# An attention and expert layer on one core: a third PSUM bank for scores, side work moved between the couples of a unit

## What is computed

```python
xn = layernorm(x)
q, k, v = xn @ Wq.T, xn @ Wk.T, xn @ Wv.T      # 16 heads of 8
q, k = rope(q), rope(k)
att = softmax(q k.T / sqrt(8)) v               # per batch and head, 512 x 512
# router, 32 experts in 8 groups of 4
scores = sigmoid(xn @ gate_w.T); sc = scores + e_bias
# keep the 4 groups with the largest sum of their top 2, then the top 6 experts
w = 2.5 * scores[top6] / (sum(scores[top6]) + 1e-20)
moe = sum_e w_e * (relu(xn @ up_e.T)**2 @ down_e.T)      # 64 wide each
shared = relu(xn @ shared_up.T)**2 @ shared_down.T       # 256 wide
out = x + att + moe + shared
```

## Time and profile before

| | |
|---|---|
| median of 3 runs | 724.7 us (721.32 to 726.27) |
| profiled execution | 720.83 us, of which the span is 719.0 |
| PE busy | 692.2 us, 96% of the span |
| DVE busy | 489.1 us, 68%; row maxima 330.9 in 512 |
| ACT busy | 407.4 us, 57%; exponents 278.0 in 512 |
| POOL busy | 397.8 us, 55% |
| mean granted clock of TensorE | 0.958 |

### The profile page before, as it was taken

The page is one execution under the profiler, slowest core; times in us unless marked ns, Lnnn a source line. Parts: engine busy times, 40 slices in busy tenths (PEclk is TensorE's granted clock), DMA queues, the critical chain, the costliest instruction groups (busy, mean ns, idle before and its releaser), DMA issues. The chain is left out here.

```text
span 719.0 us, 12483 instructions
## 1 busy us (share of the span) xinstructions
PE 692.2 (96%) x4450; PEld 326.5 (45%) x4450; DVE 489.1 (68%) x1179; ACT 407.4 (57%) x771; POOL 397.8 (55%) x337
## 2 busy tenths in 40 slices
PE   7979899999999999999999999999999999999996
PEld 7523344444544454444544454445444453445443
DVE  5872467858786788668765788668786878565400
ACT  2522445566656655566646656566656656665663
POOL 1660135665575656565654657565665555566554
PEclk9985589999999999999979999999999999999999
DMA  7816033353236334643424334643435423332320
GB/s 192 261 61 179 3 88 90 106 163 91 73 80 206 90 89 118 206 94 89 114 59 156 90 89 119 205 94 89 118 85 177 97 55 95 93 89 60 89 60 15
DMA packets 52973, 77.78 MB, mean 108 GB/s; under 512 B 6064, under 2 KB 19248, under 8 KB 52784
## 3 DMA queue, kind: packets, MB, share of 16 engines
q1 hardware_dynamic: 52336, 75.95, 40.3%
q10 hardware_dynamic: 576, 1.05, 0.4%
HBM read 57.19 MB, written 19.40 MB: 107 GB/s over the span
## 5 line engine op out<-in xcount | busy, mean ns | idle before, releaser
L629 DVE TENSOR_REDUCE nmax<-sc 128x1 f32<-128x512 f32 x512 | 330.9, 686 | 173.2 <-PE sc L799 170.5
L455 ACT ACTIVATE probs<-st 128x512 f32<-128x512 f32 x512 | 278.0, 595 | 161.3 <-PE st L815 161.2
L349 POOL TENSOR_TENSOR gated<-gate_at,relu 128x512 f32<-128x512 f32 x128 | 163.6, 1278 | 272.4 <-ACT relu L460 272.4
L832 PEld LDWEIGHTS acc<-dn,g 128*128 128x128 f32 x1024 | 136.3, 192 | 128.0 <-issue 124.9
L832 PE MATMUL acc<-dn,g 128*128 128x128 f32 x1024 | 175.8, 295 | 1.4 <-POOL g L353 1.4
L353 POOL TENSOR_TENSOR g<-gated,relu 128x512 f32<-128x512 f32 x128 | 163.0, 1273 | 18.5 <-POOL gated L349 0.4
L799 PE MATMUL sc<-stacks 32*128 32x512 f32 x512 | 154.6, 509 | 14.1 <-DVE nmax L629 12.4
L815 PE MATMUL st<-stacks 32*128 32x512 f32 x512 | 151.4, 586 | 0.0
L826 PE MATMUL pv<-probs,v_aug 128*32 128x512 f32 x1024 | 139.0, 615 | 0.0
L854 PE MATMUL upb<-xnT,up 128*128 128x512 f32 x256 | 134.0, 606 | 0.0
L460 ACT ACTIVATE relu<-upb 128x512 f32<-128x512 f32 x128 | 76.3, 596 | 83.8 <-PE upb L854 83.8
(11 more groups left out here) (107 smaller groups left out, 445.8 us busy)
## 6 DMA issues: line engine op xcount, KB each, us to landing
gate_at<-gate_rows SPq DMA_DIRECT2D x64, 512.0 KB, 6.7
q_stack<-qk_parts SPq DMA_DIRECT2D x32, 256.0 KB, 6.6
stacks<-q_stack SPq DMA_DIRECT2D x32, 256.0 KB, 3.0
stacks<-k_stack SPq DMA_DIRECT2D x32, 256.0 KB, 3.5
k_stack<-qk_parts SPq DMA_DIRECT2D x28, 256.0 KB, 5.6
gate_at<-in_x SPq DMA_DIRECT2D x8, 256.0 KB, 5.1
x_res<-in_x SPq DMA_DIRECT2D x8, 256.0 KB, 7.2
out<-y SPq DMA_DIRECT2D x8, 256.0 KB, 7.1
```

Source lines behind the costliest of these rows:

```text
L349: nc.gpsimd.tensor_tensor(gated[:, u % 2, :], gate_at[:, group % RING, u % GATES, :], relu[:, u % RELUS, :], ALU.mult).then_inc(gated_read ...
L455: nc.scalar.activation(probs[:, u % 2, h, :], st_b[h % 2][:], ACT.Exp).then_inc(probs_ready, 1)
L629: nc.vector.tensor_reduce(out=nmax[:, s % 2, at:at + 1], in_=sc_b[i % 2][:], op=ALU.max, axis=AXX, negate=True).then_inc(s_read, 1)
L832: m = nc.tensor.matmul(acc_b[:, t * P:(t + 1) * P], src[:, t * P:(t + 1) * P], weights, start=first and t == 0, stop=end, skip_group_check ...
```

## The change

- `tr` becomes a third bank for scores, `sc2`. Tile t uses bank t % 3 and waits for row maximum t-3.
- All that was written to `tr` is written to `upb`. It stands between pv and the second couple. TensorE waits before it for relu of u-1 and before up for its evacuation. ACT evacuates it between exponents 1 and 2, as it does the attention's `pv` bank.
- The attention transpose moves from kt = 2 to kt = 1, the max transpose from kt = 1 to kt = 2, shared ups to units 3 and 7, the gate transpose to 11, v to 15, the shared downs to 2 and 3. POOL's finish of a batch moves from unit 4 to 3.
- down is issued whole, behind the second couple.
- DVE: the cut stands behind the row maxima of the units with kt = 1; the attention part in the middle of them. Router pieces: 2, 3, 5 and 6 (max8 and match_replace) stand in the middle of units 3, 4, 6 and 7; 0, 1, 4, 7 and 8 at the end of units 0, 2, 4, 7 and 8. Two tensor_scalar operations move from pieces 3 and 6 to pieces 4 and 7.
- The prelude writes all transposes of x to `upb`, so that x 3 waits for the evacuation of x 2, and x 5 for that of v.

```diff
@@ banks and units
-                for n in ("sc0", "sc1", "st0", "st1", "pv", "upb", "tr", "acc")]
+                for n in ("sc0", "sc1", "sc2", "st0", "st1", "pv", "upb", "acc")]
-        V_UNIT, SH_UNIT, GATE_UNIT = 3, (7, 11), 12
-        MAX_KT, ATT_KT = 1, 2
-        SHDOWN_UNIT = (4, 5)
+        SH_UNIT, GATE_UNIT, V_UNIT = (3, 7), 11, 15
+        ATT_KT, MAX_KT = 1, 2
+        CUT_KT = 1
+        SHDOWN_UNIT = (2, 3)
-        SUM_UNIT, Y_UNIT = 2, 4
+        SUM_UNIT, Y_UNIT = 2, 3
+        ROUTE_MID, ROUTE_END = {3: 2, 4: 3, 6: 5, 7: 6}, {0: 0, 2: 1, 4: 4, 7: 7, 8: 8}
@@ ACT, a unit
-                for h in range(QUAD):
-                    exponent(u, h)
+                exponent(u, 0)
+                exponent(u, 1)
                 if kt == 0 and q:
                     att_evac(q - 1)
                 if kt == MAX_KT and q + 1 < STEPS:
                     max_rows(q + 1)
...
+                exponent(u, 2)
+                exponent(u, 3)
@@ DVE, a unit
-                for h in range(QUAD):
...
+                if n == SUM_UNIT and b:
+                    add_residual(b - 1)
+                for tile in SC_AT[u, 0] + SC_AT[u, 1]:
+                    row_max(tile)
+                if kt == ATT_KT and q:
+                    att_out(q - 1)
+                if n in ROUTE_MID and b + 1 < B:
+                    route(b + 1, ROUTE_MID[n])
+                for tile in SC_AT[u, 2] + SC_AT[u, 3]:
+                    row_max(tile)
+                if kt == CUT_KT and q + 1 < STEPS:
+                    cut_max(q + 1)
+                if n in ROUTE_END and b + 1 < B:
+                    route(b + 1, ROUTE_END[n])
@@ TensorE
-                wait(pe, s_read, tile - 1)
-                nc.tensor.matmul(sc_b[i % 2][:], stacks[rows_of(h), s % NQ, 0, qt * P:(qt + 1) * P],
+                wait(pe, s_read, tile - SC_BANKS + 1)
+                nc.tensor.matmul(sc_b[tile % SC_BANKS][:], stacks[rows_of(h), s % NQ, 0, qt * P:(qt + 1) * P],
...
             def expert_up(u):
+                b, n, kt, q = u // SLICES, u % SLICES, u % TT, u // TT
                 wait(pe, relu_ready, u)
+                if kt == ATT_KT and q:
+                    pe.wait_ge(atty_ready, q)
+                if kt == MAX_KT and q + 1 < STEPS:
+                    pe.wait_ge(m_ready, q + 2)
+                if b + 1 < B:
+                    if n in SH_UNIT:
+                        pe.wait_ge(sh_relu, (b + 1) * NSH + SH_UNIT.index(n) + 1)
+                    if n == GATE_UNIT:
+                        pe.wait_ge(gT_ready, b + 2)
+                    if n == V_UNIT:
+                        pe.wait_ge(v_ready, b + 2)
...
             for u in range(UNITS):
                 b, n, kt, q = u // SLICES, u % SLICES, u % TT, u // TT
...
+                couple(u, 0)
+                if u:
+                    pv(u - 1)
+                wait(pe, relu_ready, u)
+                if kt == ATT_KT and q:
+                    att_transpose(q - 1)
                 if kt == MAX_KT and q + 1 < STEPS:
...
                     max_transpose(q + 1)
...
                     if n in SH_UNIT:
                         shared_up(b + 1, SH_UNIT.index(n))
                     if n == GATE_UNIT:
                         gate_transpose(b + 1)
+                    if n == V_UNIT:
+                        make_v(b + 1)
+                couple(u, 2)
+                if u >= LAG:
+                    expert_down(u - LAG)
                 if n in SHDOWN_UNIT:
                     shared_down(b, SHDOWN_UNIT.index(n))
-                if u >= LAG:
-                    expert_down(u - LAG, 1)
                 expert_up(u)
```

More of the change, by code:

```diff
@@ L47 @@
 LAG = 2
+SC_BANKS = 3
 AHEAD = 12
@@ L448, in gate_out @@
                 wait(act, gate_stored, b * 16)
-                nc.scalar.activation(gT[:, :], tr_b[0:NE, :], ACT.Copy).then_inc(gT_ready, 1)
+                nc.scalar.activation(gT[:, :], up_b[0:NE, :], ACT.Copy).then_inc(gT_ready, 1)
             def exponent(u, h):
@@ L471, in _ @@
                     act.wait_ge(xnT_psum, i + 1)
-                    nc.scalar.activation(xnT[:, i * T:(i + 1) * T], turn_b(i)[:], ACT.Copy
+                    nc.scalar.activation(xnT[:, i * T:(i + 1) * T], up_b[:], ACT.Copy
                                          ).then_inc(xnT_ready, 1)
@@ L715, in transpose_x @@
                     pe.wait_ge(xn_pool, POOL_LN.index(i) + 1)
-                if i >= 2:
-                    pe.wait_ge(xnT_ready, i - 1 if i < 4 else i)
+                wait(pe, xnT_ready, i)
+                if i == 5:
+                    pe.wait_ge(v_ready, 1)
                 if i == 6:
@@ L720, in transpose_x @@
                 for t in range(TT):
-                    last = nc.tensor.transpose(turn_b(i)[:, t * P:(t + 1) * P], xn[:, i * TT + t, :], ident[:])
+                    last = nc.tensor.transpose(up_b[:, t * P:(t + 1) * P], xn[:, i * TT + t, :], ident[:])
                 last.then_inc(xnT_psum, 1)
@@ L776, in gate_transpose @@
                 for t in range(TT):
-                    m = nc.tensor.transpose(tr_b[0:NE, t * P:(t + 1) * P], gates[:, t, :], ident[:])
+                    m = nc.tensor.transpose(up_b[0:NE, t * P:(t + 1) * P], gates[:, t, :], ident[:])
                 m.then_inc(gate_turned, 1)
@@ L816, in weights_product, with couple @@
                                  stacks[rows_of(h), j, 0, :], start=False, stop=True).then_inc(t_done, 1)
+            def couple(u, h):
+                for k in (h, h + 1):
+                    weights_max(u, k)
+                for k in (h, h + 1):
+                    weights_product(u, k)
+                for tile in SC_AT[u, h] + SC_AT[u, h + 1]:
+                    score(tile)
             def pv(u):
@@ L828, in pv, with down_slice @@
                 m.then_inc(pv_done, 1)
-            def down_slice(src, weights, first, end, tiles=range(TT)):
-                for t in tiles:
+            def down_slice(src, weights, first, end):
+                for t in range(TT):
                     m = nc.tensor.matmul(acc_b[:, t * P:(t + 1) * P], src[:, t * P:(t + 1) * P], weights,
@@ L834, in down_slice, with expert_down @@
                 return m
-            def expert_down(u, half):
+            def expert_down(u):
                 b, n = u // SLICES, u % SLICES
-                if half == 0:
-                    pe.wait_ge(g_ready, u + 1)
-                    if n == 0:
-                        wait(pe, sum_ready, b)
-                last = down_slice(g[:, u % 2, :], dn[:, n, :], n == 0, n == SLICES - 1,
-                                  range(half * TT // 2, (half + 1) * TT // 2))
-                if half:
-                    last.then_inc(down_done, 1)
+                pe.wait_ge(g_ready, u + 1)
+                if n == 0:
+                    wait(pe, sum_ready, b)
+                down_slice(g[:, u % 2, :], dn[:, n, :], n == 0, n == SLICES - 1).then_inc(down_done, 1)
             def shared_down(b, i):
@@ L876, in prelude @@
                     if i == 0:
[L877 removed]
+                        pe.wait_ge(xnT_ready, 6)
                     else:
@@ L904, in _ @@
                 b, n, kt, q = u // SLICES, u % SLICES, u % TT, u // TT
-                for h in range(0, QUAD, 2):
-                    weights_max(u, h)
-                    weights_max(u, h + 1)
-                    weights_product(u, h)
-                    weights_product(u, h + 1)
-                    for tile in SC_AT[u, h] + SC_AT[u, h + 1]:
-                        score(tile)
-                    if h == 0:
-                        if u:
-                            pv(u - 1)
-                        if u >= LAG:
-                            expert_down(u - LAG, 0)
```

78 lines of the change are left out of this document (19 added, 59 removed).

## The result

The changed kernel takes 694.3 us, the median of four runs (688.47 to 699.01). The kernel before took 723.0 on the same chip (718.48 to 726.27). The ratio is 0.958, with a 95% interval of 0.949 to 0.967; it is that of the fast runs, which leaves out the run of 699.01. The prediction was 692, with a range of 668 to 712.

What follows compares the result with a forecast made beforehand. TensorE's own work was taken to bound the kernel, with score waits for DVE and clock falls on top. 719.0 - 25.7 + 2.0 - 1.7 + 0.5 - 4.5 = 689.6; 691.4 with 1.8 around, plus 1: 692, range 668 to 712.

Steps and rivals of the forecast that it cites:

- What bounds it: Whole kernel: TensorE's own work bounds it, with only scores waiting for DVE and TensorE's lower clock on top.
- The stalls removed: Third bank and moved DVE pieces remove score waits: unit 9 17.0, unit 2 4.7, rest 1.5, units 0 to 3 2.5; 25.7 us.
- DVE's residue: Unit 9's cut still ends late beside POOL, so unit 10's second couple waits: 2.0 us taken, bounds 1.2 to 8.
- list of queues: Moved DMAs, gate stores and POOL's earlier finish of a batch were claimed to delay nothing: 0.
- (D): Rival: DVE's waits only move, router pieces at five unit ends meeting POOL; 14 us lost, 705 us, chance 0.13.
- The order: TensorE's units with down whole, couple after pv and the exponents' wait: plain +0.04, max -0.1 each; net -1.7 us.
- The new wait: Second couple's maxima wait for the first couple's exponents, behind ACT's relu; its second member starts at 1.79: 0.24 us.
- Units 0 to 3 and the prelude: Score waits at half clock in units 0 to 3 go, -2.5 us; prelude transposes wait for evacuations, +0.5.
- (B): Rival: the clock also stays up through the prelude, worth 20 us: 672 us, chance 0.17.
- The clock in the steady part: The clock's fall at 368 us goes, as no array stands behind the cut: -4.5 us.
- (C): Rival: the second couple's wait costs 0.24 plus 0.55 in 67 units: 726 us, 731 with a clock fall; chance 0.10.
- (E): Rival: the change does nothing, as bank waits were hidden anyway: 719 to 725 us, chance 0.05.

Runs made afterwards that it cites:

- The best kernel: Changed kernel with POOL's splits, squares and final sum moved, v's second-buffer fills early, identity transposes of 12, 10, 12 and 8 in TensorE's stands: 668.32 us, ratio 0.9285.

## Why the prediction was right, and which of its terms were not

The span was to come out at 689.6 and came out at 692.7. That it came so close is partly luck: one term was 9.5 too small, and others were off the other way. Step by step:

- **What bounds it.** Right. The plain unit of after is TensorE's own work end to end, and with POOL moved, with no wait for DVE left, a batch is 74.55, against 74.86 for before's batch with its three stalls taken off (78.40 - 2.43 - 0.78 - 0.33).
- **The stalls removed, 25.7.** Unit 9 went from 6.85 to 4.65 and unit 2 from 5.42 to 5.18, though it now has a shared down (0.89) and a max transpose in place of the attention's: both stalls gone whole. How it came about was seen less well. The forecast books it under the third bank, and the moved pieces with it, without dividing. Two banks with the new DVE order cost 1.1 a batch at the higher clock, three banks with the old one 1.9, both together 3.4; the larger part is DVE's order.
- **DVE's residue, 2.0.** This is the term that was wrong: 11.5. Two parts. *Unit 10*: the value taken was 0.2 in six batches, the measured one 1.27, 7.6 in all, at the upper bound of 8. The step took the cut's end to be 1.2 us into unit 10, since both slow operations of the earlier trace rows got in at the first gap, each once. In the run three operations waited one after the other, each for one of three POOL operations that follow each other without a gap. The sentence "misses the gap and waits for the next one" had the right price, 1.3, and was set aside; its way there was another, one operation that waits twice. It named the wrong victim too: the max transpose waits for the cut first, at its place between the couples, not the second couple's score. *Unit 5*: 0.65 in six batches, 3.9, not in the sum at all. The change moves POOL's final sum to where piece 4 runs, and the forecast gave that move 0 in its list of queues: it asked whether the sum's inputs were there, not what it would run beside. Rival (D) had this mechanism, with "POOL is free from 3.5 to 5.0 in the new unit" against it. It is not free there in unit 4 (the final sum, 3.4 to 4.7), nor in units 6 to 9 (the splits) and 14 (a square), though only units 4 and 9 made the next one late.
- **The order, -1.7.** Right, with its working. Down whole 0.99 (1.0 forecast), pv into a couple 0.99 (no more than into a down), plain unit 4.28 (4.28), max unit 4.29 (4.32). The stall-free batch fell by 0.31, 2.4 in 7.7 batches. The bound of a whole further couple did not come: the couple takes 0.55 and the lateness, as the earlier trace rows said.
- **The new wait, 0.24.** Its size is right and its cause half so. The forecast lets ACT's relu go first; with relu behind, the exponents still end at 1.74, as they wait for the products.
- **Units 0 to 3 and the prelude.** -2.5 + 0.5 = -2.0 forecast, -6.1 measured, all of it before up of unit 0. The fall near 47 came as in the forecast, but from 63.7 to 70.5 us the clock was back. From the score at 61.24 to up of unit 0 the same work takes 10.84 us where it took 14.79 (from the score at 63.38), so the clock's return is worth 3.95 of the 6.1. Why it came back is open: before had the array shown busy in all of 60 to 70 us, and stayed at 0.50. The other 2.1 were there earlier: the score that starts at 61.24 is that much ahead of before's. With the third bank TensorE does the second shared up at 43.38, ahead of the stand and at the higher level. Before it came at 46.95, behind the stand, and took 2.04 at the lower level. The forecast saw this move, but only in (B), and gave it no price; its 2.5 were for waits in units 0 to 3. Those went too, by about the right size: units 1 to 3 take as long as before with 1.6 us more of work in them (at the higher level; more at the lower). So the 4.1 that the sum lacks are gains ahead of unit 0 that it did not price.
- **The clock in the steady part, -4.5.** Measured 4.3, in batch 3. That the fall goes with the stand was argued from one case. The experiments bear it out: all eleven falls between up 3 and up 127, in the twelve traces of this case, come at most 1.9 us after the end of a stand of 0.84 to 1.54 us, and the kernels without such a stand there have none. With the stalls gone and the stands of the start filled, the clock stays up everywhere.
- **The rivals.** (B) did not happen. TensorE did go on to the second shared up, as it says (43.38), but the score behind it came at 46.80 and had stood 2.29, not 1.7, and the clock fell. The 20 that it gave for a prelude at the higher level, on top of the forecast's 2.0, was a little high: with the stands filled, up of unit 3 comes 13.3 us sooner than in after, and 19.4 sooner than before. The best kernel's span is 14.1 below that of the kernel with POOL alone moved (681.0 to 666.9, the memset's move in it). (C) did not happen: the couple costs 0.55 and the lateness, 0.79, and a batch without stalls is shorter than before's. Its sum was also off a little: 67 x 0.55 less 1.7 is 35, not 33. The mark that the prediction set for (C), a second couple that takes longer than 0.6, was badly put, for its own forecast makes it 0.55 + 0.24 when counted from the first member (1.54) and 0.55 only from the second (1.78). (E) fell with the waits. (D) holds 11.5 of the 14 that it was priced at, though in two units instead of five, and its mark, a cut of over 1.5 us with scores behind it, was met: the cut took 3.1, with the max transpose and the scores behind it.
- **The errors cancelled in part.** 9.5 too little for the residue stands against 4.1 too little gained in the prelude and some 2.3 elsewhere in the steady part. 1.6 of the 2.3 only depend on where the line is drawn: the shared downs went from units 4 and 5 to 2 and 3, and v from 3 to 15, so batch 0 has less work behind up 3 and more in front of it. The rest, 0.7, is the order, whose stall-free batch gained 2.4 and not 1.7.
- **The median.** 1.8 around the span and 1 for a fall more would be 695.5 from the span measured; it was 694.3. The four runs of after follow the granted clock: 688.47 at 0.982, 693.97 at 0.971, 694.62 at 0.972, 699.01 at 0.961.

The Trainium skill, "SBUF — State Buffer", section "SBUF: two separate sides", had been weighed for the residue: an exclusive lock for a whole instruction. The trace agrees with each operation of the cut: 0.67, 0.97 and 1.19 end within 0.05 us of POOL's at 201.08, 202.07 and 203.30, and all four take 0.16 to 0.18 when POOL is idle. I had read the rule as one wait for one cut. It is one wait for each instruction that meets a POOL operation, and in this chain three of four did. Its section "Who interferes with whom" names copy and cast beside the operations with two inputs; the 0.67 and 1.19 are casts.

**Open.** Why the clock falls behind one stand and not behind another. In the steady part it fell once in seven stands of 0.85, five times in 24 of 1.07, once in six of 1.33 and of 1.40, and three times in six of 1.53. Ahead of up 3 it fell behind 0.65 in one kernel and not behind 1.34 in another, and in the kernel with two banks it fell at 39.9 us with no stand longer than 0.36 in the 8 us before. How much each of the fills gives was not tried one by one. Whether the work that fills a stand must be a transpose wasn't tried either.

## What to carry to other kernels

When work moves on one engine, list for each moved operation what the other engine that shares its port runs at that time: here 1.9 us a batch hung on three constants that say in which unit POOL splits, squares and sums, and moving them cost nothing. A chain of short VectorE operations beside a long row of GpSimd's must be priced per operation and not per chain. Where the array stands in a place that can't be mended, matmuls into a free bank whose results nobody uses are worth a try: 42 of them gave 14 us here, with the memset's move in it.

## What was unexpected of the hardware

- **A 0.17 us operation that takes 2.80.** VectorE's wait went over two POOL operations that had no gap between them (1.27, then a memset of 1.81), and ended 0.03 us after the second. With the memset elsewhere the same operation took 1.06. The three operations of the cut met POOL operations that followed each other as closely, and each waited for one only; what makes the difference is not shown.
- **Casts wait too.** A copy of 16 columns from float32 to bf16 took 0.67 and 1.19 beside POOL and 0.16 alone. In the earlier trace rows the two casts had fallen into gaps, so only the two subtractions had looked exposed.
- **Identity transposes in the stands kept the clock up.** With 18, 10 and 12 of them the windows from 40 to 80 us went from 0.67 to 1.00. The Trainium skill, "TensorE: Matmul & The Clock Gate", section "PE-mode transpose", says of transposes that the clock gate doesn't count them as busy in the way of other matmuls, beside a measurement in bf16. The float32 ones here don't agree with it, by these two windows; other work in their place was not tried.
- **Falls follow stands much shorter than the 2.29 of the prelude.** One came some 2 us after a stand of 0.65, one some 1 us after a stand of 1.07, with the array shown busy between the stand and the fall.
- **A group of array-wide matmuls costs 0.1 on top of its matmuls.** In down the second matmul starts 0.21 to 0.22 behind the first and the others follow at 0.11; going from half a down back to a couple costs 0.1 as well. So down takes 0.99 whole and 0.64 + 0.55 in halves.
